# Dropping the wait of the row gathers on ScalarE's copies of earlier tiles

## What is computed

```python
x = _layernorm(x + attn(x))                 # attn: layer norm, 16 heads, elu(q)+1, elu(k)+1
logits = x @ router_w                       # 14 experts
assignments = argmax(logits); weights = softmax(logits) of the chosen one
hid = gelu(x @ w1[e] + b1[e])               # 128 -> 256
moe = (hid @ w2[e] + b2[e]) * weights       # 256 -> 128, e = the token's own expert
x = _layernorm(x + moe)
```

## Time and profile before

| | us |
|---|---|
| median of 3 runs | 111.31 (111.0 to 111.91) |
| the profiled execution's own time | 110.27 |
| its span, first to last instruction | 108.5 |
| busy: PE 80.3, POOL 63.8, DVE 62.8, ACT 57.6 | |
| mean granted TensorE clock | 0.929 of full speed |

### The profile page before, as it was taken

The page is one execution under the profiler, slowest core; times in us unless marked ns, Lnnn a source line. Parts: engine busy times, 40 slices in busy tenths (PEclk is TensorE's granted clock), DMA queues, the critical chain, the costliest instruction groups (busy, mean ns, idle before and its releaser), DMA issues.

```text
span 108.5 us, 2212 instructions
## 1 busy us (share of the span) xinstructions
PE 80.3 (74%) x606; PEld 68.5 (63%) x606; DVE 62.8 (58%) x258; ACT 57.6 (53%) x180; POOL 63.8 (59%) x109
## 2 busy tenths in 40 slices
PE   5987999999996976629775665788999989940000
PEld 4864979889885964416564665687997969720000
DVE  4799996746588877940000504133588776888600
ACT  0425894865498999700222616375565758724110
POOL 6768799900013869237774463751066888877770
PEclk9999999999999999855899999999999999999555
DMA  2929999200000005407775776411000110111110
GB/s 43 362 98 330 366 294 291 76 3 1 0 0 9 0 0 195 163 32 234 252 242 179 222 256 207 146 53 29 0 0 24 30 48 27 48 48 51 48 48 24
DMA packets 9674, 12.16 MB, mean 112 GB/s; under 512 B 1426, under 2 KB 7230, under 8 KB 9662
## 3 DMA queue, kind: packets, MB, share of 16 engines
q1 hardware_dynamic: 8276, 9.69, 27.4%
q0 software_dynamic: 1024, 2.11, 6.6%
q10 hardware_dynamic: 362, 0.23, 0.9%
HBM read 6.07 MB, written 2.11 MB: 75 GB/s over the span
## 4 chain that ended last, share of the span: by engine, by line
PE 47%; DVE 17%; POOL 10%; issue 9%; DMA 7%; ACT 5%; POOLq 1%; DVEq 1%; another core or an unknown queue 0%
PE ps_o L1015 13%; POOL out L529 9%; PE ps_k L1015 8%; PE ps_q L1015 8%; PE ps_a L1015 6%; PE ps_r L1015 4%; DMA x_sb<-L_attn_x 3%; DMA acc<-x_rows,source 3%; ACT hid L692 2%; DVE acc L965 2%; PE ps_t L1025 2%; ACT k_parts L697 2%; DVE stats L775 2%; PE ps_r L1238 1%; POOLq L70 1%
## 5 line engine op out<-in xcount | busy, mean ns | idle before, releaser
L510 POOL DMA_INDIRECT acc<-x_rows,source x16 | 16.2, 1013 | 13.3 <-ACT xs_t L687 5.0
L965 DVE SCALAR_TENSOR_TENSOR acc<-ps_o,share,acc 128x128 f32 x29 | 10.2, 351 | 23.5 <-PE ps_o L1015 17.7
L1015 PE MATMUL ps_o<-w_sb,hid 128*128 x116 | 19.1, 287 | 6.2 <-ACT hid L692 2.2
L1015 PEld LDWEIGHTS ps_o<-w_sb,hid 128*128 128x128 f32 x116 | 15.2, 191 | 8.3 <-issue 8.0
L529 POOL DMA_INDIRECT out<-k_parts,source x16 | 15.9, 996 | 4.4 <-issue 4.1
L382 POOL TENSOR_TENSOR rstd<-ve,exponent 128x4 f32<-128x4 f32 (+3 forms) x14 | 12.5, 892 | 8.8 <-DVE ve L1003 6.3
L692 ACT ACTIVATE hid<-ps_q,shared 128x128 f32<-128x128 f32 x30 | 9.3, 364 | 7.5 <-PE ps_k L1015 3.7
L692 ACT ACTIVATE hid<-ps_k,shared 128x128 f32<-128x128 f32 x28 | 8.7, 364 | 8.5 <-PE ps_k L1015 3.0
L697 ACT ACTIVATE k_parts<-acc,shift,rstd 128x128 f32<-128x128 f32 x15 | 7.0, 489 | 8.3 <-DVE shift L987 4.4
L1015 PE MATMUL ps_q<-xs_t,shared 128*128 (+1 forms) x60 | 10.3, 293 | 0.4 <-issue 0.4
L1015 PE MATMUL ps_k<-xs_t,shared 128*128 x56 | 9.6, 294 | 0.8 <-issue 0.8
(11 more groups left out here) (205 smaller groups left out, 194.8 us busy)
## 6 DMA issues: line engine op xcount, KB each, us to landing
shared<-w_sb SPq DMA_DIRECT2D x29, 129.0 KB, 2.3
w_sb<-L_ffn_w SPq DMA_DIRECT2D x1, 1792.0 KB, 7.3
x_rows<-rows SPq DMA_DIRECT2D x4, 258.0 KB, 2.1
x_sb<-L_attn_x SPq DMA_DIRECT2D x4, 256.0 KB, 4.1
acc<-x_rows,source POOLq DMA_INDIRECT x16, 2.7
out<-k_parts,source POOLq DMA_INDIRECT x16
wqkv_sb<-L_attn_Wqkv ACTq DMA_DIRECT2D x1, 192.0 KB, 3.8
wo_sb<-L_attn_Wout SPq DMA_DIRECT2D x1, 64.0 KB, 4.6
```

Of the source, the lines that this page charges most:

```text
L510: pool.indirect_dma_start(acc[:, t, :], None, x1_rows, bass.IndirectOffsetOnAxis(ap=source[:, t:t + 1], axis=0), bounds_check=last_token, ...
L965: dve.scalar_tensor_tensor(out=tile, in0=ps_y[j % 2], scalar=share[:].rearrange("p t e -> p (t e)")[:, bass.ds(t_of[j] * ROW + j, 1)], in1 ...
L1015: return pe.matmul(o, l, r, start=start, stop=stop)
```

## The change

From the fifth gather on, POOL waited before each gather t until ScalarE had copied turned tile t - 4 (`px_ok` at t - 3). Those two lines are gone; POOL issues the 16 gathers one behind the other once `x1_rows` is written and `source` is known.

```diff
             pool.wait_ge(x1_out, 16 * NC)
             pool.wait_ge(source_ok, 1)
             for t in range(NT):
-                if t >= 4:
-                    pool.wait_ge(px_ok, t - 3)
                 pool.indirect_dma_start(acc[:, t, :], None, x1_rows,
                                         bass.IndirectOffsetOnAxis(ap=source[:, t:t + 1], axis=0),
                                         bounds_check=last_token, oob_is_err=False).then_inc(acc_in[t], 16)
```

## The result

| | before | after |
|---|---|---|
| median of the runs | 111.61 us (4 runs, 111.0 to 112.72) | 120.17 us (4 runs, 119.54 to 120.91) |
| ratio | | 1.0825, interval 1.0771 to 1.0878 |
| the profiled execution and its span | 110.27, 108.5 | 119.96, 118.2 |
| mean granted clock of PE | 0.929 | 0.869 |

The change makes the kernel 8% slower, outside the predicted range and on the other side of no change.

The account below looks back on a forecast made before the run. PE was taken to bound the kernel, with the time of hidden(13) setting the end. Terms of -1.0 and +0.3 sum to -0.7 us, taking the median 111.31 to 110.6 us, range 107.6 to 112.8.

Parts of the forecast that it names:

- When gathers are issued: On POOL: gathers come 1.30 us apart, the last starting at 67.75 instead of 72.64; worth nothing to POOL itself.
- The end moves with hidden(13), one for one: At the tail: finished tiles, last step and POOL's scatters shift by whatever the change takes off hidden(13), then at 75.70 us.
- The gather wait on the path: On PE before turn(14): the 0.51 us wait for gather 14 goes; by dependencies alone the gain is 0.2 us.
- The steps that run with no gather about: From hidden(10) to hidden(13): three steps at 1.07 us instead of 1.41, a gain of 1.0 us that contains the 0.2.
- What the gathers do where they move to: From 57.4 to 68.7 us: 9 gathers instead of 6 beside the weight copies; cost between 0 and 1.0, taken as 0.3 us.
- 4.8 us to be had: From hidden(4) to hidden(13) on PE: 9 steps in 14.44 us where 9.63 would do; the most that could be gained.
- the slower rival: Without pauses until 68.7 us every gelu may come late, 3.0 us a step: +1.7, or 113.0 us; chance 0.21.
- nothing but the dependency: Rival: late gelus and late steps stay, only 0.2 us at turn(14) goes; 111.1 us, chance 0.22.

Follow-up runs that it names:

- later copies: Changed kernel with SP's weight copy j, from j = 8 on, waiting until PE has done hidden(j - 8); 119.18 us, ratio 1.065 on chip B.
- window of 8: Kernel before with its wait loosened: gather t waits for the copy of tile t - 8, from t = 8 on; 107.14 us, ratio 1.0083.
- the paced one: Changed kernel with two small POOL operations behind every gather from the fourth on; 109.75 us on chip A, 110.94 us on chip B.
- windows of 3, 5 and 8: Kernel before with gather t waiting for the copy of tile t - 3, t - 5 or t - 8; ratios 1.0039, 1.0177 and 1.0083.

## Why the prediction was wrong

**What is shown.** In this kernel, gathers issued 1.30 us apart without a pause hold up the results of PE's products, on every chip but A. The changed kernel did it in the first result, on chip B and on chip C, by 12.12, 12.57 and 11.19 us of idle PE; on chips D and E kernels made from it did. Spacing the gathers at 1.72 us takes the long hole away (9.6 us on chip B), 1.53 does not (chip C), and without gathers no result is late at all (chip C). It ends with the gathers: with gathers 1.30 us apart the last held gelu starts 3.7 to 4.1 us behind the last gather's start (71.73 behind 67.89; 72.26 behind 68.31; 71.92 behind 68.11; 72.05 behind 68.39), or 3.0 without the copies. In the changed kernel that is 1.5 us after the last landing (71.73 and 70.23). Releases in between occur (66.84 with later copies, 63.88 without copies), and the next result is held again. The late gelus of before look like the same thing in small: without gathers no gelu is late and the kernel takes 103.4 us. POOL's wait on `px_ok` was thus a brake: a late tile copy kept the next gather back until the held results had come through.

**What stays open.** What in the chip the gathers and PE's results contend for. The copies, the DMA load, the loading of code, register addresses and DVE are each excluded as the sole cause; short signals between engines and PSUM only as far as 12 rounds go. Float32 products alone, outside this kernel, weren't measured. Nor is it known why chip A is free of it; only its window of 8 and its kernel without copies show that it is.

The traces show one more thing, and no run tests it: records of semaphore events are missing just where results are late. Each landing adds 16 to its semaphore, so 16 gathers should leave 256 events. The trace has 256 of them in chip A's kernel without copies and 240 in its window of 8, but 32 in the first result, 36 on chip B and 32 on chip C for the changed kernel, and 64 in the paced one on chip B. From 60 to 70 us the changed kernel's first trace holds 18 semaphore events of any kind, where the window of 8 has 370 and the kernel with plain loads 321 on chip A and 319 on chip C. Every execution timed here has a recorded span and clock, so none shows how long the kernel takes without recording, and whether the recording has a part in the hold-up is open. It also means that "issue" and "remote" in these stretches can stand for a record that is missing.

**The steps of the prediction.**

- *When gathers are issued*: right. 1.30 apart, the last at 67.89 (67.75 forecast), ending at 68.89 (68.74), and worth nothing to POOL.
- *The end moves with hidden(13), one for one*: right. hidden(13) +9.55, the last scatter 104.62 to 114.31, +9.69.
- *The gather wait on the path*: right. turn(14) waits for no gather any more.
- *The steps that run with no gather about*, -1.0: nearly right, but behind the loss. hidden(10) to hidden(13), 81.91 to 85.25 us, take 3.34 us instead of 4.22, which is -0.88: a step that still holds a turn takes 1.11 us, and the 1.07 was read where only the first step has one. From hidden(4) to hidden(13) there are now 11.64 us where there were 14.44. Of these, (2.13 - 1.11) + (1.72 - 1.11) = 1.6 are the half clock behind 12.12 us of idle PE, which the prediction hadn't in it at all.
- *What the gathers do where they move to*: **this step failed.** I bounded its cost by 1.0 us and took 0.3, from a mean pace of 2.05 us a step. Measured: hidden(4) at 73.61 instead of 61.26, a cost of 12.35. Then -2.80 for the steps behind it gives the 9.55. In the terms of the sum, hidden(10) comes at 81.91 instead of 71.48, so what was put at 0.3 came to 10.43.

The sum was therefore wrong in one bound. The mean of 2.05 was taken over a stretch in which the gathers still paused (0.99 us before 58.15 and 1.80 before 60.94), and I carried it over to ten us without a pause. The rows spoke against a constant pace: gelu(2) came through at 59.90, in the second of these pauses. The agreement of 4.70 us of holes with 4.8 us to be had was chance: the hole of 1.26 lies before hidden(4), and from there on the holes make 3.44. What I had as an observation in the slower rival ("after each pause the first results of PE reach ACT at once") says that with no pause there may be no release until the end; its price was then again a pace, 3.0 a step, and 1.7 us, a sixth of what came. The rival, with a chance of 0.21, was right in mechanism and side and wrong in size; no rival reached the 120.17 us measured.

I also read the fall from 1.88 to 1.53 us a step as the copies' doing. The experiments say the opposite: on chip C the kernel with gathers and no copies took 116.62 us, the one with all copies and no gathers 103.39, with PE never held. The Trainium skill, "SBUF — State Buffer", section "SBUF: two separate sides", which the rival "nothing but the dependency" names, says that DMA and compute don't slow each other. By that the stretch from 58.50 of the kernel without gathers is as it should be (PE full beside 236 GB/s), and the one with gathers and no copies isn't explained.

*No version found beats the kernel before on every chip.* The paced kernel is 0.9895 of before (0.978 to 1.001) on chip B and 1.0252 on chip A; windows of 3, 5 and 8, each on one chip, are even with before or slower. Of the versions that do the same work, the best left is before itself.

## What to carry to other kernels

A wait that guards no data can still be a brake that some transfer needs; before taking it out, ask what becomes dense without it, and if no row shows that density for as long as it would last, widen the range or measure it first with a paced version. Where the profile calls the end of a wait "remote" or "issue" right behind another engine's finished work, ask whether the signal itself was late, and don't price that by a mean over a stretch with pauses. Compare such kernels on more than one chip, and make sure that a control lasts as long as what it stands in for: the plain loads here were over before the long hole began.

## What the runs showed of the hardware

- Row gathers of 128 rows by POOL cost 1.00 us each and 0.30 between them. Idle time of ACT before a held gelu, at most: 13.49 us at 1.30 apart (first result), 5.65 at 1.53 (chip C), 2.25 at 1.72 (chip B). Beside 16 plain loads of the same rows' size, 0.55 apart for 8.8 us, and behind them, no gelu was held up.
- Beside them, 12 rounds between DVE and ACT took 0.36 us each and 12 between PE and ACT 0.45.
- SP's issues of copies with a register address go from 0.65 to about 2.2 us apart under dense gathers (first result); with constant addresses they stay at 0.65 but for one gap of 2.3 (chip E). On chip A, in the window of 8, they stay at 0.65 with registers too, but for one gap of 1.0.
- Behind the hole of 12.12 us, PE ran at a granted clock of 0.56 for 3.85 us, its group of four matmuls taking 1.17 us instead of 0.66.
- Chips differ: one kernel took 105.23 us on one and 116.62 on another, while the kernel without gathers took 103.40 and 103.39.
